# Gated cross-attention block on one core: VectorE without a loop, and work reordered in three kinds of step of the attention and at the start of the gate product

## What is computed

```python
# x (4,1024,512), ctx (4,64,512): 16 heads of 64, causal mask, weights rounded in blocks of 32
def attention(query, key, value, w_q, w_k, w_v, w_o):
    scores = jnp.einsum('bhqd,bhkd->bhqk', q, k) * SCALE + (1.0 - mask) * -10000.0
    out = jnp.einsum('bhqk,bhkd->bhqd', softmax(scores), v)
    return out.reshape(bsz, q_len, HEADS * HEAD_DIM) @ w_o

def ffn(x, w_gate, w_up, w_down):
    x = act_qdq(x)
    up = act_qdq(x @ lpbq_dequant(w_up).T)
    gate = act_qdq(x @ lpbq_dequant(w_gate).T)
    gate = act_qdq(gate * fixed_qdq_u16(sigmoid(gate)))
    return act_qdq(gate * up) @ lpbq_dequant(w_down).T

x = x + tanh(g_xattn[0]) * attention(layernorm(x), ctx, ctx, w_q, w_k, w_v, w_o)
x = x + tanh(g_ffn[0]) * ffn(layernorm(x), w_gate, w_up, w_down)
```

## Time and profile before

| | us |
|---|---|
| median of three runs | 1481.16 (1479.95 to 1481.19) |
| the profiled execution | 1489.47 |
| its span, first to last instruction | 1487.7 |
| mean granted TensorE clock | 0.952 |
| PE busy in the span | 1329.8 (89%) |
| DVE busy | 1034.5 (70%) |
| ACT busy | 644.7 (43%) |
| POOL busy | 259.7 (17%) |

### The profile page before, as it was taken

The page is one execution under the profiler, slowest core; times in us unless marked ns, Lnnn a source line. Parts: engine busy times, 40 slices in busy tenths (PEclk is TensorE's granted clock), DMA queues, the critical chain, the costliest instruction groups (busy, mean ns, idle before and its releaser), DMA issues. The chain is left out here.

```text
span 1487.7 us, 18885 instructions
## 1 busy us (share of the span) xinstructions
PE 1329.8 (89%) x6142; PEld 1090.9 (73%) x6142; DVE 1034.5 (70%) x1397; ACT 644.7 (43%) x769; POOL 259.7 (17%) x312
## 2 busy tenths in 40 slices
PE   7899999999999978999999999999992019999999
PEld 6778777777877856888888778877882018888887
DVE  0379669767966655777777679999998984545453
ACT  3334334333333214333334255556667973333331
POOL 1024224213412220001000035541020000000000
PEclk9999999999999998999999999999996559999999
DMA  8003212312322435766664889986558963444543
GB/s 311 1 22 114 79 43 92 99 42 71 102 75 82 171 112 204 247 238 238 247 240 157 272 295 308 317 312 208 174 197 335 318 228 116 161 166 151 175 144 118
DMA packets 111248, 259.77 MB, mean 175 GB/s; under 512 B 10832, under 2 KB 23120, under 8 KB 109648
## 3 DMA queue, kind: packets, MB, share of 16 engines
q1 hardware_dynamic: 110896, 259.04, 50.2%
q10 hardware_dynamic: 288, 0.00, 0.0%
HBM read 152.04 MB, written 106.95 MB: 174 GB/s over the span
## 5 line engine op out<-in xcount | busy, mean ns | idle before, releaser
L1097 PE MATMUL gpG<-xph,Wh 128*128 128x512 f32 x384 | 153.2, 399 | 6.0 <-DVE xpl L1021 6.0
L1571 PE MATMUL pD<-Wh,xph 128*128 128x512 f32 x384 | 150.5, 392 | 4.6 <-DVE xpl L1550 4.6
L1097 PE MATMUL pU<-xph,Wh 128*128 128x512 f32 x384 | 150.6, 392 | 2.2 <-ACT ust L1222 1.2
L1097 PE MATMUL gpG<-xph,Wl 128*128 128x512 f32 x384 | 150.8, 393 | 0.0
L1097 PE MATMUL gpG<-xpl,Wh 128*128 128x512 f32 x384 | 150.7, 392 | 0.0
L1097 PE MATMUL pU<-xpl,Wh 128*128 128x512 f32 x384 | 150.3, 391 | 0.0
L1571 PE MATMUL pD<-Wh,xpl 128*128 128x512 f32 x384 | 150.3, 391 | 0.0
L1097 PE MATMUL pU<-xph,Wl 128*128 128x512 f32 x384 | 150.2, 391 | 0.0
L1571 PE MATMUL pD<-Wl,xph 128*128 128x512 f32 x384 | 150.2, 391 | 0.0
L1550 DVE TENSOR_TENSOR xpl<-doq,xph 128x1536 fp32r<-128x1536 int16 (+1 forms) x34 | 56.4, 1663 | 122.4 <-ACT xph L1517 122.4
L1004 ACT ACTIVATE gst<-gpG,sc 128x512 f32<-128x512 f32 x96 | 66.3, 691 | 168.8 <-PE gpG L1097 168.8
(11 more groups left out here) (172 smaller groups left out, 2884.0 us busy)
## 6 DMA issues: line engine op xcount, KB each, us to landing
dub<-up_d SPq DMA_DIRECT2D x42, 768.0 KB, 4.7
gate_d<-gst SPq DMA_DIRECT2D x96, 256.0 KB, 2.3
gb<-gate_d SPq DMA_DIRECT2D x32, 768.0 KB, 6.0
up_d<-ust SPq DMA_DIRECT2D x96, 256.0 KB, 4.1
xr<-xn_d SPq DMA_DIRECT2D x9, 1024.0 KB, 6.0
xph<-up_d SPq DMA_DIRECT2D x11, 768.0 KB, 6.3
xpl<-up_d SPq DMA_DIRECT2D x11, 768.0 KB, 6.2
xin<-in_x SPq DMA_DIRECT2D x32, 256.0 KB, 2.6
```

The lines of the kernel that those rows point to most:

```text
L1097: mm = pe.matmul(ps[:, :], Ws[:, it, kt * P:(kt + 1) * P], xs[:, kt, :], start=(kt == 0 and Ws is Wh and xs is xh), stop=(kt == KT - 1 and ...
L1571: mm = pe.matmul(pD[4 * t + q][:, :], os_[n][:, cs], Ws[:, it, :], start=(it == 0 and os_ is oh and Ws is Wh), stop=(it == IT - 1 and os_ ...
```

## The change

Six edits, in the attention unless said otherwise:

1. `schedule` gets a switch; DVE's list of the three looped batches is written out, the other engines keep their loop.
2. ACT runs `job_hi` first in the A-chunk step, before the two copies pTh.
3. DVE's `residual` is cut in two: `residual` now makes x1 alone, `statistics2` its sums. In the A-chunk step DVE's order becomes x1, `job_lo`, pTl, `statistics2`, `statistics`, `scores_down`.
4. In the last batch's steps 8 to 10 DVE runs `scores_down`, x1, pTl, `statistics2`.
5. PE runs `turn_x` first in the steps with k % 8 == 2.
6. At the start of the gate phase ACT makes each integer piece and its high part in turn, where it made four and then four.

```diff
-        def schedule(eng, step):
+        def schedule(eng, step, straight=False):
             for k in range(-2, 3):
                 step(0, k, lambda j: j >= 0, False)
-            with eng.Fori(0, B - 1) as b:
-                for k in range(3, BQ + 3):
-                    step(b, k, lambda j: True, True)
+            if straight:
+                for b in range(B - 1):
+                    for k in range(3, BQ + 3):
+                        step(b, k, lambda j: True, True)
+            else:
+                with eng.Fori(0, B - 1) as b:
+                    for k in range(3, BQ + 3):
+                        step(b, k, lambda j: True, True)
...
# ACT
+                q = job_at(k, jobs, 2)
+                if q is not None and which == 0:
+                    job_hi(act, J, b, q)
                 if have(k - 2):
...
-                q = job_at(k, jobs, 2)
-                if q is not None:
+                if q is not None and which != 0:
                     job_hi(act, J, b, q)
...
# DVE
+                q = job_at(k, jobs, 2)
+                if which == 0:
+                    sums_up()
+                    if q is not None:
+                        job_lo(dve, J, b, q)
+                    lows()
+                    spread2()
+                    normal()
+                    down()
+                elif k >= 3 and not have(k):
+                    down()
+                    sums_up()
+                    lows()
+                    spread2()
+                else:
+                    normal()
+                    lows()
...
-            schedule(dve, step)
+            schedule(dve, step, straight=True)
...
# PE
+                if k % BQ == 2:
+                    turn_x()
+                if have(k - 2):
...
-                turn_x()
+                if k % BQ != 2:
+                    turn_x()
                 values(b, k, have)
...
# ACT, gate phase
-            parts(0, 0)
             for kt in range(KT):
+                integer(0, 0, kt)
                 high(0, 0, kt)
```

More of the change, by code:

```diff
@@ L664, in residual, with statistics2 @@
                                          op0=ALU.mult, op1=ALU.add).then_inc(x1_done, 1)
+            def statistics2(b, j):
+                n = j % 2
                 dve.wait_ge(*tile(x1_done, b, j))
@@ L690, in some @@
                         chunks.pop(0)()
[L692 to L700, removed]
@@ L701, in step, with lows @@
-                q = job_at(k, jobs, 2)
[L702 to L711, removed]
+                def lows():
+                    if have(k - 2):
+                        j = k - 2
+                        for h, cs in enumerate(halves):
+                            dve.wait_ge(*part(pTh_done, b, j, h))
+                            dve.tensor_tensor(pTl[:, cs], pT[:, cs], pTh[:, cs].bitcast(F32), ALU.subtract).then_inc(pTl_done, 1)
@@ new lines, in down, with sums_up, spread2, normal @@
+                def down():
+                    if have(k - 1):
+                        scores_down(b, k - 1)
+                def sums_up():
+                    if have(k - 3):
+                        residual(b, k - 3)
+                def spread2():
+                    if have(k - 3):
+                        statistics2(b, k - 3)
+                def normal():
+                    if have(k + 2) and k + 2 >= 2:
+                        statistics(b, k + 2)
+                q = job_at(k, jobs, 2)
@@ new lines, in step @@
+                if which == 0:
[14 more added lines that the diff above has]
+                    lows()
+                    if q is not None:
+                        job_lo(dve, J, b, q)
+                    early = which is not None or not have(BQ)
+                    if early:
+                        sums_up()
+                        spread2()
+                    down()
+                    if not early:
+                        sums_up()
+                        spread2()
@@ L808, in step @@
                 which, ahead = matrices(k, have)
[L809 to L819, removed]
                 def turn_x():
@@ L831, in turn_x @@
                         mm.then_inc(xT_ps, 1)
+                if k % BQ == 2:
+                    turn_x()
+                if have(k - 2):
+                    j = k - 2
+                    pe.wait_ge(*tile(prob_done, b, j))
+                    pe.wait_ge(*part(pTl_done, b, j - 1, 1))
+                    for p in range(PAIRS):
+                        if k % BQ == 2 and p % 4 == 0:
+                            pe.wait_ge(*at(ch_lo, NCH * b, NCH * (k // BQ) + NCH - 1 + p // 4))
+                        mm = pe.transpose(pT[:, p * P:(p + 1) * P], pr[j % 2][:, p * P:(p + 1) * P], ident[:, :])
+                        if p % 4 == 3:
+                            mm.then_inc(pT_ps, 1)
                 if which != 0 and have(k) and k >= 0:
                     scores(b, k)
-                turn_x()
+                if k % BQ != 2:
+                    turn_x()
                 values(b, k, have)
@@ L978, in _, with integer @@
         def _(act):
-            def parts(i, T):
+            def integer(i, T, kt):
                 n = T % 2
[L982 to L986, removed]
+                if T:
+                    act.wait_ge(*turned(i, T, kt))
+                    act.wait_ge(*at(xl_done, 2 * KT * i, KT * (T - 2) + kt + 1))
+                act.activation(xq[n][:, kt, :], pX[kt][:, :], ACT.Copy, scale=INV_X).then_inc(xq_done, 1)
             def high(i, T, kt):
@@ L1005, in evictions @@
                         if it == 4 and not (last and t):
-                            parts(i, t + 1)
+                            for kt in range(KT):
+                                integer(i, t + 1, kt)
                         if it in range(5, 5 + KT) and not (last and t):
```

## The result

The changed kernel takes 1462.58 us (median of four, 1460.32 to 1463.74) against 1481.18 us before. The ratio is 0.986, 95% interval 0.9838 to 0.9883: 18.6 us faster where 21.5 had been forecast. The profiled execution took 1460.32 us, its span is 1458.4 us. The span thus lost 29.3 us, some eleven more than the median, which has to be explained too; PE's busy time, for the same products, is 1317.7 us instead of 1329.8.

What follows compares the result with a forecast made beforehand. PE was taken as the bound, busy 89% of the span, so only its waits or own work count. Terms 5.9 + 5.7 + 1.1 + 7.3 + 1.5 = 21.5 us, from the 1481.16 us median, gave 1460 us, range 1454 to 1469.

Steps and rivals of the forecast that it cites:

- The A-chunk step, 5.9 us: Three A-chunk steps, edits 2 and 3: earlier job split shortens PE's 3.48 us wait; gain 5.9 us, between 2 and 9.
- the new wait: A-chunk step, before the third piece of A: PE waits 2.1 us for a low part of A.
- the 7.6 of the text: Forecast gain of the three A-chunk steps before 1.7 us was charged for one fall in clock.
- the second rival: Timed runs had no low clock to give back: A-chunk steps give 1.8, all 13.5 us, 1467.7; chance 0.12.
- a fall behind the new wait: A-chunk steps: one drop to PE's lower clock in the three steps, charged at 1.7 us.
- The ends of batch, 5.7 us: Two ends of batch, edit 1: without DVE's 5.27 us stall PE's x1 waits go; 5.7 us, bounds 4.1 to 5.8.
- My lengths: DVE's attention list: written out, some 230 instructions longer; POOL's and ACT's loops little over half DVE's length.
- PE's turn of x, 1.1 us: Steps with k = 10 and step 2, edit 5: turn falls into V wait; 1.1 us, between 0 and 1.4.
- The drain, 7.3 us: Last batch, edit 4: no wait for probabilities, 1.1 us waits, full clock; 7.3 us, bounds 5.0 and 7.5.
- The gate's start, 1.5 us: Gate phase start, edit 6: first high part directly behind first integer, PE starts 1.5 us earlier; bounds 0.8 and 1.6.

Runs made afterwards that it cites:

- the second profile of before: The kernel before, unchanged, profiled and timed again: span 1482.0 us, median 1483.36 us, ratio 1.0004.
- the two comparisons: The changed kernel against the kernel before, timed first (1462.58 us, ratio 0.986) and again unchanged (1463.99 us, ratio 0.9871).
- two more moves: Changed kernel with, in the A-chunk step, ACT's xn behind six high parts of A and DVE's maximum, subtraction and two low parts before the sums: 1453.88 us, 0.9818.

## Why the prediction was right, and where a term was not

The gain of 18.6 us lies inside the range (12 to 27) and 3 us under the sum. By the steps of the sum:

- **The A-chunk step, 5.9 us.** The mechanism came out nearly to the tenth: turn of x after a wait of 0.70 (0.65 forecast), third piece 8.60 us behind the job (8.7), the new wait 1.76 (2.1). Against the first profile of before the three steps gained 19.63 + 20.66 + 19.64 - 3 x 17.44 = 7.6 us, the 7.6 of the text. The size is where it was off: 5.8 of these are low clock, which the second profile of before has once and the first three times. At full clock the edit is worth 1.8 us, the number that I gave to the second rival. Undoing it cost 5.9 by the median, so the typical execution lies between. That my 5.9 comes near is in part luck: it took 5.8 us of one execution's low clock for the step's own and charged 1.7 for a fall behind the new wait, which came in none of the three steps of the first profile and in one of the second.
- **The ends of batch, 5.7 us.** 2 x 2.5 at full clock, 4.6 for the edit alone. No stall in straight code, no jump of POOL or ACT behind it. The rule of the Trainium skill ("Runtime: NRT & Kernel Launch", Instruction fetch mechanics), that a branch taken to a target outside the two pages held waits for a fetch, agrees in kind: stalls of 5.3 to 5.5 us at each taken jump of this loop, none at its third end, where the list runs on, and none in straight code. My lengths left out the semaphore instructions: by all that the trace holds the loops of DVE, ACT and POOL have 261, 141 and 135 instructions, and DVE's attention list is 810 long written out where it was 445, some 365 more and not 230. It didn't stall all the same. The 108 ns of the Trainium skill's "Advanced Engine Details and Errata", Control Flow Timing, are not what this jump took.
- **PE's turn of x, 1.1 us.** 0.45 us a batch against 0.24, by the traces alone; x1 held nothing back.
- **The drain, 7.3 us.** 22.72 to 15.46 is 7.3. Both waits 1.13 (1.1 forecast), none for the probabilities, full clock.
- **The gate's start, 1.5 us.** 11.58 to 10.02 is 1.6.

The step that failed is the one that tied the sum to the profiled execution: I took its low clock as a fixed part of the kernel, and explained the 8.3 us between it and the three timed runs by nothing. The 24 executions spread over 15 us; this one was high. The sum was then taken from the median of the timed runs, which hold less of it; that the two came within 3 us of each other is in part luck. The second rival read the same gap as if the timed runs had no low clock at all. In hindsight the nearest single number is the sum of waits (15.0 us: 8.3 for the job's low part, 6.4 for x1 and pTl, 2.3 for the probabilities, 1.3 for V and 1.7 at the gate, less 5.0 for A) plus some 4 us, a part of the low clock of the first profile. Do the edits add? The medians of the undone ones add to 23.8 us (9.8 + 5.9 + 5.9 + 1.1 + 1.1), the ratios to 19.2, about the whole gain (18.6 and 19.4 us by the medians of the two comparisons); so it isn't shown that they bring more together than singly. One sign of it is in the traces: behind the new wait of 1.8 us the clock fell in 4 of the 6 A-chunk steps of the two kernels with DVE's loop back, and in 1 of 15 elsewhere. Why isn't settled.

## What to carry to other kernels

Where one engine is the bound, list its waits, chain each engine's rows by hand through the new order; here the waits so found were right to 0.4 us or better. Look in the same chain for the wait that the new order makes, since here it cost 5.3 us and two more moves took it away. Keep what follows a wait in granted clock as a separate term with its own spread, and profile the kernel before twice before pricing it. A long loop body on an engine that others wait for can be written out to lose the stall of its jump, if its trace shows one: DVE's loop of 261 instructions did, its loop of 196 didn't.

## What the runs showed of the hardware

A jump back in DVE's attention loop (261 instructions in the trace) left DVE idle by issue for 5.3 to 5.5 us in the profiles of every kernel that kept it, while ACT's and POOL's loops of 141 and 135 instructions, and DVE's own of 196 in the gate phase, showed no idle time by issue at theirs. The branch itself lasts 0.05 to 0.08 us in the trace.

Low clock behind waits of 1.8 to 3.5 us came and went from one execution to the next. In the twelve further profiles and the two of before and after, the wait of 3.4 to 3.5 us in the A-chunk step was followed by PE's lower level in 9 of 15 steps; the new wait of 1.8 us in 5 of 21; the same step with 1.4 us or none in 0 of 6; the waits of 2.0 to 2.5 us at the ends of batch in 5 of 10; and the three waits of 2.3 us within 14 us in the drain in 4 of 4. A fall cost PE 1.6 to 1.7 us, and 2.3 to 2.7 us in the second A-chunk step of the first profile of before (20.66 for 18.03), in all three with edits 2 and 3 undone (20.75) and in the drain (7.92 for 5.57). The same wait did and didn't bring it in executions of one and the same kernel: 3 of 3 A-chunk steps in the first profile of before, 1 of 3 in the second, 0 of 3 with edit 4 alone, whose list is the same there. The steps of one execution need not be independent of each other, so these counts are rough.
